# Local attention on Trainium2: score products of 64 rows, and both cosine products on GpSimd

## The reference, cut to what matters

```python
def attn_layer(x, Wqkv, qs, ksc, Wo):          # 16 heads of 64, windows of 32 tokens
    q, k, v = split(x @ Wqkv)                  # 128 -> 3 * 1024
    q = l2norm(q) * qs;  k = l2norm(k) * ksc
    q = q * cos * scale + rotate_half(q) * sin * scale
    k = k * cos / scale + rotate_half(k) * sin / scale
    # each window of 32 queries looks at its own 32 keys and the 32 before them
    sim = einsum('bhwie,bhwje->bhwij', bq, bk2) * 8, masked
    out = einsum('bhwij,bhwje->bhwie', softmax(sim), bv2)
    return out @ Wo
```

## Time and profile before

| | |
|---|---|
| median of 3 runs | 4704.75 us (4704.15 to 4711.61) |
| the profiled execution | 4695.61 us, its span 4693.8 us |
| mean granted TensorE clock | 0.953 |
| TensorE matmul, weight loads | 86%, 66% of the span |
| VectorE | 80% |
| ScalarE | 65% |
| GpSimd | 43% |
| DMA engines | 19 GB/s on average |

### The profile page before, as it was taken

The page is one execution under the profiler, slowest core; times in us unless marked ns, Lnnn a source line. Parts: engine busy times, 40 slices in busy tenths (PEclk is TensorE's granted clock), DMA queues, the critical chain, the costliest instruction groups (busy, mean ns, idle before and its releaser), DMA issues. The chain is left out here.

```text
span 4693.8 us, 116229 instructions
## 1 busy us (share of the span) xinstructions
PE 4058.7 (86%) x42352; PEld 3115.0 (66%) x42352; DVE 3754.1 (80%) x7533; ACT 3051.5 (65%) x4888; POOL 2034.4 (43%) x1420
## 2 busy tenths in 40 slices
PE   5988988989989889938858689899899898898898
PEld 4866857857758768616535478578577587686685
DVE  7988979979979889845335389799799798798897
ACT  5866857848848758612413478488488487586685
POOL 5544536535536545320010155265355365354452
PEclk9999999999999999967968899999999999999999
DMA  1000000000000000040030000000000000000000
GB/s 51 9 24 14 8 31 7 9 29 9 23 14 9 22 17 8 6 95 2 1 81 2 25 17 9 30 8 8 28 9 23 14 9 22 15 9 24 13 8 13
DMA packets 30619, 88.78 MB, mean 19 GB/s; under 512 B 7504, under 2 KB 13648, under 8 KB 28368
## 3 DMA queue, kind: packets, MB, share of 16 engines
q1 hardware_dynamic: 29104, 80.95, 6.4%
q10 hardware_dynamic: 1152, 3.15, 0.3%
HBM read 38.72 MB, written 1.05 MB: 8 GB/s over the span
## 5 line engine op out<-in xcount | busy, mean ns | idle before, releaser
L780 POOL TENSOR_TENSOR pool<-pool 128x512 f32<-128x512 f32 x768 | 1177.1, 1563 | 1147.0 <-DVE pool L878 1147.0
L450 PE MATMUL psum<-squares,pool 128*128 128x128 f32 x3072 | 710.0, 278 | 66.3 <-POOL pool L784 35.6
L452 PE MATMUL psum<-squares,pool 128*128 128x128 f32 x3072 | 700.2, 275 | 0.0
L492 PE MATMUL psum<-wqkv_hi,xs_lo 128*128 128x512 f32 x1152 | 514.0, 446 | 110.4 <-DVE pool L878 45.5
L867 DVE TENSOR_REDUCE pool<-pool 128x16 f32<-128x1024 f32 x384 | 453.4, 1216 | 177.9 <-ACT pool L694 174.6
L483 PE MATMUL psum<-pool 128*64 128x128 f32 x6144 | 539.5, 289 | 61.7 <-ACT pool L670 54.7
L655 ACT COPY pool<-psum 64x512 f32<-64x512 f32 x768 | 447.3, 582 | 215.2 <-PE psum L452 209.9
L450 PEld LDWEIGHTS psum<-squares,pool 128*128 128x128 f32 x3072 | 432.7, 141 | 149.3 <-issue 61.1
L670 ACT COPY pool<-pool 32x512 f32<-32x512 f32 x768 | 486.7, 634 | 9.0
L694 ACT ACTIVATE pool<-psum 128x1024 f32<-128x1024 f32 x384 | 376.5, 1023 | 171.6 <-PE psum L494 167.7
L493 PE MATMUL psum<-wqkv_lo,xs_hi 128*128 128x512 f32 x1152 | 461.7, 401 | 0.0
(11 more groups left out here) (167 smaller groups left out, 8172.0 us busy)
## 6 DMA issues: line engine op xcount, KB each, us to landing
pool<-pool SPq DMA_DIRECT2D x192, 128.0 KB, 2.3
pool<-in_wqkv SPq DMA_DIRECT2D x12, 1536.0 KB, 6.1
k_st<-turn_st SPq DMA_DIRECT2D x8, 1536.0 KB, 21.4
pool<-in_wo SPq DMA_DIRECT2D x12, 512.0 KB, 3.5
pool<-in_w SPq DMA_DIRECT2D x12, 341.0 KB, 3.0
pool<-in_w SPq DMA_DIRECT2D x12, 192.0 KB, 2.8
rotary<-in_rotary SPq DMA_DIRECT2D x2, 1024.0 KB, 5.1
pool<-in_scale SPq DMA_DIRECT2D x12, 128.0 KB, 6.6
```

The costliest lines, as they stand in the source:

```text
L450: pe.matmul(o, by_cos[:, p // 2, 2 * c:2 * c + 2, :], ident, start=True, stop=False, is_transpose=True)
L452: last = pe.matmul(o, by_sin[:, p // 2, 2 * c:2 * c + 2, :], ident, start=False, stop=True, is_transpose=True)
L492: pe.matmul(o, xs_lo[:, k % 2, :], wqkv_hi[:, c], start=True, stop=False)
L780: last = g.tensor_tensor(by_sin[:, q, :, hd * r:hd * r + hd], qn[:, q, :, hd * (1 - r):hd * (2 - r)], tab, ALU.mult)
```

## The change

Three things, all in the local layers. (1) The keys are kept without zeros, `kT[pair][keys]`, and copied by one instruction of 128 rows; the carry of the last 32 keys (L762) copies half as many elements. (2) Each score product takes one head: 64 rows, 32 query columns, 64 key columns; the even head lies in rows 0 to 63 of the array and writes bank 4, the odd one in rows 64 to 127 and writes bank 5. There are twice as many products. The heads stand in another order in the scores, which `values` undoes by its index. (3) The cosine product of q leaves VectorE, where it stood between the residual and `less_top`, and stands on GpSimd between the sine products of q and those of k. A semaphore increment is added on PE's queue twice per unit; one of SyncE's is taken out per layer.

```diff
-            kT = [cut(PAIRS, 2, WIN + P) for _ in range(2)]
+            kT = [cut(PAIRS, WIN + P) for _ in range(2)]
...
     PE, turned_scores:
                             for c in range(PAIRS):
                                 if c % 4 == 0:
                                     pe.wait_ge(t_out, done(U, 4, 2 + c // 4))
+                                    plain(pe)
                                 for w in range(NW):
-                                    o = bank(4 + c // 4)[WIN * w:WIN * w + WIN, P * (c % 4):P * (c % 4) + P]
-                                    last = pe.matmul(o, qT[:, c, WIN * w:WIN * w + WIN],
-                                                     kT[k % 2][:, c, :, WIN * w:WIN * w + 2 * WIN],
-                                                     start=False, stop=(c % 4 == 3))
+                                    for r in range(2):
+                                        rows = slice(64 * r, 64 * r + 64)
+                                        o = bank(4 + r)[WIN * w:WIN * w + WIN, 2 * WIN * c:2 * WIN * c + 2 * WIN]
+                                        last = pe.matmul(o, qT[rows, c, WIN * w:WIN * w + WIN],
+                                                         kT[k % 2][rows, c, WIN * w:WIN * w + 2 * WIN],
+                                                         start=False, stop=(c == PAIRS - 1))
...
     PE, values:
-                                r = 64 * (h % 2)
+                                r, at_h = 64 * (h % 2), PAIRS * (h % 2) + h // 2
...
     ScalarE, turned:
-                                for r in range(2):
-                                    last = a.copy(kT[k % 2][64 * r:64 * r + 64, c:c + 4, r, WIN:WIN + P],
-                                                  bank(7 - p % 2)[64 * r:64 * r + 64, :]
-                                                  .rearrange("p (c t) -> p c t", c=4))
-                                last.then_inc(t_out, 1)
+                                a.copy(kT[k % 2][:, c:c + 4, WIN:WIN + P],
+                                       bank(7 - p % 2).rearrange("p (c t) -> p c t", c=4)).then_inc(t_out, 1)
...
     GpSimd, keep and step:
-                            g.tensor_copy(b[:, :, :, 0:WIN], b[:, :, :, P:P + WIN]).then_inc(k_kept, 1)
+                            g.tensor_copy(b[:, :, 0:WIN], b[:, :, P:P + WIN]).then_inc(k_kept, 1)
...
                                     last.then_inc(sin_ready, 1)
-                                tab = turn[:, bass.ds(t, 1), 1, :].broadcast_to([P, HEADS, DH])
-                                g.tensor_tensor(by_cos[:, 1], qn[:, 1], tab, ALU.mult).then_inc(k_cos_ready, 1)
+                                    tab = turn[:, bass.ds(t, 1), q, :].broadcast_to([P, HEADS, DH])
+                                    g.tensor_tensor(by_cos[:, q], qn[:, q], tab, ALU.mult).then_inc(cos_ready, 1)
...
     VectorE, step:
-                                v.wait_ge(k_cos_ready, done(U - 1))
-                                v.wait_ge(cos_ready, done(U - 1))
+                                v.wait_ge(cos_ready, done(U - 1, 2, 1))
...
-                                if k == 0:
-                                    v.wait_ge(turn_ready, done(l + L0))
-                                v.wait_ge(qn_ready, done(U, 2, 1))
-                                v.wait_ge(t_ready, done(U - 1, 4, 1))
-                                tab = turn[:, bass.ds(t, 1), 0, :].broadcast_to([P, HEADS, DH])
-                                v.tensor_tensor(by_cos[:, 0], qn[:, 0], tab, ALU.mult).then_inc(cos_ready, 1)
```

More of the change, by code:

```diff
@@ L123, in plain @@
         def plain(eng):
-            eng.sem_inc(passed_sp if eng is nc.sync else passed_pool, 1)
+            eng.sem_inc(passed_sp if eng is nc.sync else passed_pe if eng is nc.tensor else passed_pool, 1)
         def rsqrt(v, x, tmp, step, first, op0, c0, op1, c1, between=()):
@@ L312, in tables @@
             def tables(eng, layer):
-                eng.wait_ge(cos_ready, done(layer * UNITS - 1))
-                eng.wait_ge(k_cos_ready, done(layer * UNITS - 1))
+                eng.wait_ge(cos_ready, done(layer * UNITS - 1, 2, 1))
                 eng.wait_ge(sin_ready, done(layer * UNITS - 1, 2, 1))
@@ L406, in _ @@
                         sp.wait_ge(sin_ready, done(last, 2, 1))
-                        plain(sp)
-                        sp.wait_ge(cos_ready, done(last))
-                        sp.wait_ge(k_cos_ready, done(last))
+                        sp.wait_ge(cos_ready, done(last, 2, 1))
                         plain(sp)
@@ L433, in turned_scores @@
                             pe.wait_ge(sin_ready, done(U, 2, 0))
-                            pe.wait_ge(cos_ready, done(U))
+                            pe.wait_ge(cos_ready, done(U, 2, 0))
                             if isinstance(i, int) and i == 0 and k == 0:
@@ L443, in turned_scores @@
                                     pe.wait_ge(sin_ready, done(U, 2, 1))
-                                    pe.wait_ge(k_cos_ready, done(U))
+                                    pe.wait_ge(cos_ready, done(U, 2, 1))
                                 if p >= 2:
@@ L480, in values @@
                             for h in range(HEADS):
-                                r = 64 * (h % 2)
+                                r, at_h = 64 * (h % 2), PAIRS * (h % 2) + h // 2
                                 o = bank(6 + h // 8)[r:r + 64, P * (h // 2 % 4):P * (h // 2 % 4) + P]
-                                pe.matmul(o, V[k % 4][:, DH * h:DH * h + DH], pT[:, h, :], start=True, stop=False)
+                                pe.matmul(o, V[k % 4][:, DH * h:DH * h + DH], pT[:, at_h, :], start=True, stop=False)
                                 last = pe.matmul(o[:, 0:WIN], v_last[k % 2][:, DH * h:DH * h + DH],
-                                                 pT_last[:, h, :], start=False, stop=True)
+                                                 pT_last[:, at_h, :], start=False, stop=True)
                             last.then_inc(o_ready, 1)
@@ L862, in step @@
                             if has(0):
-                                t = 2 * i + k // 2
                                 for q in range(2):
```

7 lines of the change are left out of this document (3 added, 4 removed).

## The result

The kernel after took 4769.12 us (4754.06 to 4782.81), the kernel before 4704.45: the ratio is 1.0149, 95% interval 1.0132 to 1.0166. It is slower by 65 us, 1.5%, where I had forecast 10 us less. The profiled execution took 4754.06 us.

A forecast was written before the change was run, and what follows sets the result against it. ACT bounded steady units at 16.0 us; a DVE/POOL loop of 15.65 would follow. Per layer +0.95, -2.3 and +0.9 make -0.45; twelve layers -5.4, two without a next -4.8: about -10 from 4704.75, so 4695 us, range 4650 to 4815.

The forecast's parts named there:

- Scores: PE's score products per unit: 128 half-width instructions take 1.0 us against 1.9, 3.8 as the slow end.
- the room: PE's queue: its own work falls from 15.4 to about 14.5 us, leaving slack for the two added semaphore increments.
- my rivals: Whole kernel: first small step held (0.22), score products not overlapping (0.08), small steps less blocked by POOL (0.12).
- Slip: DVE's first small step meets POOL's sixth product, held to 9.8 us: 16.3 us per unit, about +104 us; chance 0.22.
- The pace: Local units from the second on: 15.65 us each against 16.0 in steady ones; fourteen take 219.9, -2.3 per layer.
- the loop's ends: Ends of the unit loop in each layer: an estimated 0.8 us added to 14 x 15.65.
- The first small step: DVE's first inverse-root step on 128x32 elements (L145 of before) slips in as POOL's fifth product ends, some 0.3 us.
- the second: DVE's second such step (L146 of before) is held until POOL's sixth product ends, some 1.8 us in every unit.
- ACT waits for DVE's transposes: Sign on ACT ahead of its diagonal copies: it waits for DVE (L833) before L665, not for PE.
- First interval: First to second unit start of a layer, without softmax between: 13.6 us instead of 12.67, +0.95.
- Copies of the keys: ACT's key copies: two pairs of 1.18 us become two single copies of 0.59, 1.18 us less in ACT's loop.
- The layer's end: Next weights' load issued 1.35 us later, after the last cosine product of k: +0.9 us per layer.

The follow-up runs named there:

- a_unroll: The kernel after with PE's inner loop over the 12 middle units of a local layer written out, for PE alone: 4695.27 us, 0.9985 of before.
- b_unroll: The kernel before with PE's inner loop written out in the same way, as the control: 4696.73 us, 0.9985 of before.
- d_unroll: The kernel before with the key and score part of the change only, and PE's inner loop written out: 4603.41 us, 0.9801 of before.
- p_more4: The kernel before with one product in values issued once more for 4 of 16 heads, 1701 PE instructions a pass: 4873.44 us, one run.
- q_shift256: The kernel before with 256 semaphore increments on PE ahead of its inner loop, the loop itself unchanged: 5165.32 us, one run.

## Why the prediction was wrong

**The failed step** is "Scores" of the change part by part. It priced 128 instructions in place of 64 by how they run (rounds of so many ns) and gave PE "the room"; it did not ask where they stand, and the wait for instructions at the loop's return is a term that the sum has at nothing. PE's inner loop stood at most 26 instructions short of the cliff in the first six layers, and the change added 516 (2153 - 1637). The two returns in a layer, with the unit behind each (7th, 8th, 11th and 12th interval, after less `a_unroll`), cost 2.78 + 0.73 + 2.53 + 0.72 = 6.8 us a layer, 81 us over twelve by the profiled executions' intervals. (As a whole these two executions differ by 52 us and the medians by 74: the stretches between layers, 91 to 102 us each, scatter by some us.) That turned a forecast of 10 us less into 65 more. None of my rivals had it; that the result fell into the range was luck, owed to the Slip's price and not to its mechanism. What I should have looked at was there: the instruction queue on the page of the profile, with 209 packets for a program of which most stands in loops, and the number of PE's instructions in a pass.

**The rest of the sum, by steps, against `a_unroll`,** where that wait is gone:

- *The pace.* Forecast 15.65 from the second unit on and 0.8 us for the loop's ends, 219.9 for the fourteen; measured (234.46 - 13.54) = 220.9, that is 15.78 each: the term was right, a little low. The first small step at 0.3 and the second at 1.8 us came as written (0.25 and 1.81). ACT waits for DVE's transposes ahead of `diagonal`, 0.96 us, as forecast.
- *First interval.* Forecast 13.6, measured 13.54.
- *Slip.* It occurs as single units: an interval of 16.3 to 16.5 near the start of some layers (L144 held 2.2 to 2.4 us) and, in the kernel after, the unit behind each stall (16.5; L144 comes 9 us after the start and is held 0.9 to 1.3 us). It never becomes the regime.
- *Scores.* Taken 1.0 us, bounds 0.9 to 3.8. The row above has 128 in 1.61 us against 64 in 1.96: between the bounds, 0.35 less instead of 0.96. Less the last one's 0.22 us, they start 1.39 / 127 = 11 ns apart on average, so the 25 ns of the Trainium skill that I cited do not hold between tiles side by side. At 15.0 of 15.7 us PE was not the bound.
- *Copies of the keys.* One copy of 128 rows in 0.59 us, as forecast.
- *The layer's end.* Forecast +0.9 a layer for the later load. From a layer's last unit to the next layer's first the stretches are 93 to 97 us before and 91 to 97 after (the one with the global attention left out): the term can't be read from them, and stays open.

In sum `a_unroll` stands at 4695.27 us, which is my number, in part by luck; against `b_unroll`, the fair partner, it is no change at all (4696.73), where I had -10.

**What I priced but did not separate.** I knew that the DVE/POOL loop of 15.65 us would set the pace and that ACT's would have been 14.85. I did not work out the scores part alone. It would have shown what the cosine part does: DVE, freed of 2.2 us, waits 1.8 us at the second small step, which ends 10.17 us after a unit's start in `a_unroll` and 9.85 in `d_unroll`, where it is not held: 0.3 us, the difference between their paces (15.74 and 15.46). The time taken off DVE comes back as blocking.

## What to carry to other kernels

Count the instructions in the body of an engine's loop before and after an edit: a body near the size that the engine can hold falls off a cliff that no busy share shows, its mark is idle time with releaser "issue" on the first instruction of each pass, with a packet of the instruction queue inside it, and writing the loop out cured it here. The number of packets alone is no mark: written-out loops raised it too, without a pause. The place of the loop in its engine's program counts as well as its length. Cost each half of a change alone, against the bound that it would leave: here a gain of 93 us and a loss of 92 us arrived as one diff. Work moved to GpSimd beside VectorE's small SBUF steps cost here what its product boundaries cost: put short products where the small steps come.

## What the runs showed that I had not expected

- A pause of 3.75 us on PE is followed by more than 5 us at a granted clock of 0.50, and the next unit is 0.7 us longer; yet the interval with the pause grows by 2.8 us only, since PE has slack and the others catch up.
- It cost more where PE had less slack: with pauses of about the same length (4.0 and 3.9 us on average) the 7th interval grows by 2.8 us in the kernel after (PE's work 15.0 of 15.7 us), by 5 in `p_more4` (20.89 against 15.9), which has PE's old scores. That the slack is the reason fits, but no run varied it alone.
- Instructions ahead of a loop can decide whether it stalls: 64 of them brought the stall to a pass of 1637, 168 took it from a pass of 1701.
- A semaphore increment on PE took 0.15 us (median from one start to the next in `q_shift256`); 256 of them made the interval (51.33 - 15.39) / 256 = 0.14 us longer for each, as PE had some slack.
- PE's loop over the layers pauses as well, before and after alike: the branch at its ten returns lasts 3.3 to 4.0 us in both traces, its two exits 0.07 us. No run took these pauses away, so what they cost is open.
